# GpSimd's last loop: scatter-adding block b before gathering block b + 4

## What is computed

```python
x = x + xattn(layernorm(x), ctx_1024, ctx_1024, ...)
xf = layernorm(x).reshape(-1, 256)                    # 2048 tokens
top_w, top_idx = top_k(xf @ gate_w, 2)                # two experts per token
combine = zeros((2048, 8)).at[rows, top_idx].add(softmax(top_w))
h = gelu(einsum('td,edf->tef', xf, w1) + b1)          # 8 experts, 256 -> 1024
y = einsum('tef,efd->ted', h, w2) + b2                # 1024 -> 256
x = x + einsum('ted,te->td', y, combine)
```

## Time and profile before

| | |
|---|---|
| time before, median of 3 runs | 368.38 us (356.95, 368.38, 372.02) |
| the profiled execution's own time | 358.27 us |
| its span | 356.5 us |
| busy in the span | TensorE 316.4, VectorE 260.8, ScalarE 236.4, GpSimd 174.2 us |
| the 39 scatters on GpSimd (L486) | 64.8 us busy, 109.6 us idle just before them |
| the 39 gathers on GpSimd (L479) | 41.3 us busy, 37.4 us idle just before them |
| DMA queues, share of 16 engines' span | q1 (SyncE) 52.5%, q0 (GpSimd) 17.3% |

### The profile page before, as it was taken

The page is one execution under the profiler, slowest core; times in us unless marked ns, Lnnn a source line. Parts: engine busy times, 40 slices in busy tenths (PEclk is TensorE's granted clock), DMA queues, the critical chain, the costliest instruction groups (busy, mean ns, idle before and its releaser), DMA issues.

```text
span 356.5 us, 11376 instructions
## 1 busy us (share of the span) xinstructions
PE 316.4 (89%) x3919; PEld 289.6 (81%) x3919; DVE 260.8 (73%) x604; ACT 236.4 (66%) x543; POOL 174.2 (49%) x189
## 2 busy tenths in 40 slices
PE   6589888889977999999999899999989999999940
PEld 4478787888867999998999789889889899999930
DVE  8989998971798888877778767777768765666600
ACT  1589989972333688877888858678777564656510
POOL 7878989942103154444544453535442635444231
PEclk9999999975786999999999999999999999999985
DMA  7899999999411068598787876877777778778221
GB/s 232 267 348 330 351 352 334 330 392 322 159 10 46 17 167 279 176 278 251 204 258 205 268 182 202 235 244 202 244 205 233 223 233 220 246 217 267 37 29 15
DMA packets 34096, 78.52 MB, mean 220 GB/s; under 512 B 10437, under 2 KB 23945, under 8 KB 27514
## 3 DMA queue, kind: packets, MB, share of 16 engines
q1 hardware_dynamic: 24088, 66.72, 52.5%
q0 software_dynamic: 7600, 10.48, 17.3%
q10 hardware_dynamic: 2354, 0.59, 0.7%
HBM read 31.07 MB, written 9.64 MB: 114 GB/s over the span
## 4 chain that ended last, share of the span: by engine, by line
PE 58%; DVE 8%; DMA 8%; issue 6%; ACT 3%; POOL 2%; POOLq 1%; DVEq 0%; ACTq 0%
PE bank L1090 25%; PE bank L1105 23%; DMA out<-shared,row_of 6%; PE bank L1066 2%; DVE W L874 1%; PE bank L1007 1%; PE bank L1031 1%; DVE shared L926 1%; DMA shared<-xn_rows,row_of 1%; PE bank L1057 1%; PE bank L963 1%; PE bank L1107 1%; PE bank L988 1%; PE bank L957 1%; PE bank L996 1%
## 5 line engine op out<-in xcount | busy, mean ns | idle before, releaser
L486 POOL DMA_INDIRECT out<-shared,row_of x39 | 64.8, 1662 | 109.6 <-DMA out<-shared,row_of 74.6
L1105 PE MATMUL bank<-W,shared 128*128 (+1 forms) x936 | 108.5, 273 | 0.0
L1090 PE MATMUL bank<-shared,XR 128*128 128x128 f16 x1680 | 99.9, 218 | 5.0 <-issue 4.0
L1090 PEld LDWEIGHTS bank<-shared,XR 128*128 128x128 f16 x1680 | 95.8, 97 | 8.4 <-issue 8.0
L1105 PEld LDWEIGHTS bank<-W,shared 128*128 128x128 f16 x936 | 89.9, 98 | 9.8
L604 ACT ACTIVATE shared<-shared 128x512 f32<-128x512 f32 x78 | 49.1, 629 | 53.4 <-DVE shared L926 53.0
L945 DVE SCALAR_TENSOR_TENSOR shared<-shared,XP 128x512 f16<-128x512 f32 x70 | 52.4, 749 | 25.8 <-ACT shared L606 25.3
L926 DVE SCALAR_TENSOR_TENSOR shared<-bank,XP 128x512 f32<-128x512 f32 x70 | 52.5, 750 | 24.1 <-PE bank L1090 20.3
L479 POOL DMA_INDIRECT shared<-xn_rows,row_of x39 | 41.3, 1059 | 37.4 <-DVE w_of L941 14.0
L606 ACT ACTIVATE shared<-shared,XP 128x512 f16<-128x512 f32 x70 | 50.6, 723 | 2.3
L874 DVE SCALAR_TENSOR_TENSOR W<-W,wscale (+1 forms) x32 | 40.8, 1280 | 2.9 <-ACT W L538 1.5
(11 more groups left out here) (169 smaller groups left out, 422.2 us busy)
## 6 DMA issues: line engine op xcount, KB each, us to landing
XR<-W SPq DMA_DIRECT2D x35, 1024.0 KB
W<-in_w SPq DMA_DIRECT2D x16, 1024.0 KB, 7.5
shared<-in_ctx_t SPq DMA_DIRECT2D x16, 256.0 KB, 5.2
W<-in_ctx SPq DMA_DIRECT2D x16, 128.0 KB, 6.3
out<-XR SPq DMA_DIRECT2D x16, 128.0 KB, 6.3
xn_rows<-W SPq DMA_DIRECT2D x16, 128.0 KB, 6.4
XR<-in_x SPq DMA_DIRECT2D x3, 512.0 KB, 7.3
shared<-xn_rows,row_of POOLq DMA_INDIRECT x39, 4.2
```

Source lines behind the costliest of these rows:

```text
L486: pool.indirect_dma_start(out=out, out_offset=bass.IndirectOffsetOnAxis(ap=row_of[:, b:b + 1], axis=0), in_=Y[:, b % 2, :], in_offset=None ...
L1090: mm = pe.matmul(pHT[n][m][:, f % 4, :], first[:, c, w, f * P:(f + 1) * P], XT[:, n, v, c, :], start=(c == 0 and w == 0 and v == 0), stop= ...
L1105: pe.matmul(pY[n], hT[:, n, v, f, :], whole(Wh[:, slot, at:at + D]), start=(f == 0 and w == 0 and v == 0), stop=False)
```

## The change

In GpSimd's loop the two halves of the body change places. At each index i the scatter of block i - 2 is now issued first, and the gather of block i + 2 after it. Both keep their waits. In terms of blocks, the gather of block b + 4 used to come ahead of the scatter of block b (and behind that of block b - 1), and now comes behind the scatter of block b.

```diff
             for i in range(-2, NB + 2):
-                b = i + 2
-                if b < NB:
-                    after(pool, gt_ok, b - 2)
-                    after(pool, got_w, b - 2)
-                    pool.indirect_dma_start(out=XG[:, b % 3, :], out_offset=None, in_=xn_dram,
-                                            in_offset=bass.IndirectOffsetOnAxis(ap=row_of[:, b:b + 1], axis=0))\
-                        .then_inc(xg_ok[b % 3], 16)
                 b = i - 2
                 if 0 <= b:
                     after(pool, added, 16 * b)
                     pool.wait_ge(ys_ok, b + 1)
                     pool.indirect_dma_start(out=out,
                                             out_offset=bass.IndirectOffsetOnAxis(ap=row_of[:, b:b + 1], axis=0),
                                             in_=Y[:, b % 2, :], in_offset=None, compute_op=ALU.add,
                                             bounds_check=ROWS - 1, oob_is_err=True).then_inc(added, 16)
+                b = i + 2
+                if b < NB:
+                    after(pool, gt_ok, b - 2)
+                    after(pool, got_w, b - 2)
+                    pool.indirect_dma_start(out=XG[:, b % 3, :], out_offset=None, in_=xn_dram,
+                                            in_offset=bass.IndirectOffsetOnAxis(ap=row_of[:, b:b + 1], axis=0))\
+                        .then_inc(xg_ok[b % 3], 16)
```

## The result

The changed kernel is slower by a quarter: 458.98 us in the median of 4 runs (450.18 to 465.96), against 363.01 us (356.95 to 372.02, 4 runs). The ratio to the kernel before is 1.264, with a 95% interval of 1.245 to 1.284. The forecast was 369.5 us and the range 359 to 384.

The account below looks back on a forecast made before the run. The prediction took TensorE to bound the block loop. Steady stage +5.9, start +3.4 and end -3.1 us sum to +6.2 us, which on the median of 363.3 us gives 369.5 us; range 359 to 384.

Parts of the forecast that it names:

- The loop: Transposes, product, Y, scatter, gather behind it, landing, transposes two blocks on: (8.53 + L) / 2, so 6.02 us per block.
- half of the stalls: TensorE's stalls, 0.25 us a block, would add 0.125 if all stayed; half was taken, giving 6.08 us a block.
- The landing, L: Time from a gather's issue to its landing, meeting the first part of the next copy: taken as 3.5 us.
- The prediction's own sign of being wrong, a landing over 4: In the block loop, a gather's landing over 4 us would show the forecast wrong.
- The rival with L at 4.2 us: Gather latency sets the block loop's pace in full: +16.6 to +20.3 us, about 5% slower; chance 0.25.
- the fit of the Trainium skill: GpSimd-issued DMA takes 2.0 us plus bytes over 436 GB/s: gather 2.3 us, no cost in the steady stage.
- The reaction: GpSimd's step from Y done to the scatter's issue: 0.29 us.
- The clock: Rival: waits of 0.2 to 0.5 us a block lower TensorE's clock for a tenth of the stage, +19 us; chance 0.03.
- The start: Blocks up to 7: block 7's transposes come at 149.17 against 145.80 before, +3.4 us.
- The end: Last scatters no longer lag: the last one 16.60 us after the last transposes, 19.69 before, -3.1 us.
- Faster: Rival: TensorE's stalls vanish under the waits in the block loop, -2.2 us, at most -8 us; chance 0.05.
- The loop stays slack: Rival: landings of 3.1 us, 5.82 us a block, TensorE keeps its pace, within 3 us of before; chance 0.17.

Follow-up runs that it names:

- nobounds: The changed kernel with the scatter's bounds check left out: 456.21 us, ratio 1.256.
- hold: The changed kernel with SyncE's 1 MB copy of w1 held back until the scatter of four blocks before has landed: 404.44 us, ratio 1.116.
- fill: The changed kernel with 48 small unused matmuls on TensorE ahead of the transposes of every even block from 4 on: 434.83 us, ratio 1.196.
- both: The changed kernel with the held copy and the filler matmuls together: 416.15 us, no ratio.

## Why the prediction was wrong

**The bound and the loop were right.** The loop, its seven steps, its unit of two blocks, and that the scatters all but stop waiting for each other and land faster (3.8 us in the median, 5.0 before) came as written. The profile shows the landing of the scatters:

```profile
DMA to landing us min/median/max: 3.7/3.8/6.7
```

**What the gather meets, and what the wait does to the clock, were wrong, all to one side.** The prediction had 12.03 us for two blocks, plus 0.12 for half of the stalls. The turn followed above has 16.84:

| term | predicted | measured |
|---|---|---|
| transposes to bias matmul | 5.53 | 7.97 (246.41 to 254.38) |
| bias matmul to Y done | 0.78 | 0.79 |
| Y done to scatter | 0.29 | 0.89 (255.17 to 256.06) |
| scatter to gather | 1.89 | 1.89 |
| gather's landing, and start | 3.54 | 5.30 |

*The landing, L.* This is the step that failed first. The text took L = 3.5 for a gather issued "some 0.7 us ahead of the next copy", which "meets its first part". No run bears that out. The late gathers of the changed kernel take 5.3 to 5.8 us, those of nobounds that go out 0.45 to 0.76 us ahead of the copy 5.7 to 6.1: they land with the copy. The prediction's own sign of being wrong, a landing over 4, was met. The price 3.5 came from the gathers of 253.38 and 322.89 in the kernel before (3.4 and 3.7), said to have "the nearest" surroundings. The copies behind those two show that they had not:

```profile
255.60 0.49 SPq L371 DMA_DIRECT2D XR<-W  x1
325.98 0.49 SPq L371 DMA_DIRECT2D XR<-W  x1
```

They went out 2.2 and 3.1 us behind the gathers, not 0.7. The rival with L at 4.2 us was too low as well. The run hold, in which the copies go out 2.0 us or more behind most gathers again, shows that the copy is the cause (3.0 to 3.1 us in the turns shown), and takes the ratio from 1.264 to 1.116, more than half of the loss.

The phase was off too, but that made no difference. I had stretched each iteration by the forecast wait; the wait stands ahead of every second transposes only, and the other iteration begins 0.10 us after the product. So the scatter goes out 1.58 us into it (254.48 to 256.06), not 0.5 to 0.7.

By the fit of the Trainium skill that the prediction names, an estimated 2.3 us of landing would have made the change free in the steady stage. The least landing here is 2.8 us in the changed kernel, and 5.3 beside a copy of SyncE. "DMA: Bandwidth & Descriptors" of the Trainium skill, section "Queues, rings and completion order", says that each DMA engine takes turns between the queues that have work for it, a packet at a time. The runs agree in this much, that a gather on q0 isn't served ahead of a copy on q1 that is in flight beside it, even where the gather was issued first: 5.3 to 5.8 us, against 3.0 to 3.1 in the turns of hold.

*The reaction.* I took 0.29 us from one row at the end of the kernel before. That scatter (343.48) wasn't set off by its Y alone: in the chain that ended last the scatter before had landed at 342.64, 0.84 us ahead of it, and GpSimd was already on its way when Y was done at 343.19. In the steady stage of the changed kernel it needs 0.89 us from Y to scatter, 0.56 of it as "issue" ahead of its last semaphore. This term is 0.6 us too small, but since the gather lands with the copy whether it goes out some tenths earlier or later, no run shows that it cost anything in the changed kernel; where the copy is out of the way, as in hold, it counts in full.

*The clock.* I gave it 3%, as a rival by itself, for pauses of 0.2 to 0.5 us. The pauses are 3.5 us, since the gather lands so late. TensorE's part of the loop grows by 2.44 us. Of these 1.6 are the slower w1 matmuls (4.45 us, 2.86 before), and the run fill took them away and with them some 20 us. The other 0.8 us are the later start of the w1 matmuls, 1.05 us after the transposes in place of 0.22. It is there in fill as well, so it isn't the clock; its cause is open. The prediction had let half of such stalls vanish under the new waits. The run both shows that copy and clock are no sum of independent cases: I should have put them into one rival in which one brings on the next.

*The start.* Predicted +3.4 us up to block 7, measured +13.7: the first turn is long already (block 4's transposes come 10.87 us after block 3's).

*The end.* Predicted -3.1 us, measured +0.5. In hold and fill the last scatter comes 17.56 and 17.76 us after the last transposes, 19.69 in the kernel before, so 2 us are gained there and the mechanism was right. In the changed kernel it takes 20.18: its last w1 matmuls follow a wait and are slow.

*The chances.* Slower had 0.40, no change 0.55. The range came from the median landing and bounded it by no collision, although the prediction itself quoted landings up to 5.2 us for gathers and 6.8 for scatters. Small slips change nothing: with L = 3.1 the start would be +2.6 and not +3.0, and the idle time in the earlier trace rows is 5.2 and not 5.4 us. The fit of the Trainium skill, an estimated 5.42 us a block by the loop, would end at TensorE's own 5.64 and so under "Faster", not under "The loop stays slack".

## What to carry to other kernels

A prefetch that is issued behind a result's write inherits every wait of that result, and closes a loop through the engine that it feeds. Work out the loop in the order in which the consumer really runs: where it carries over two iterations, one of them starts late and the other on time, and the transfer's phase against others must be taken for the one that starts on time. Here a small gather issued within a microsecond of a 1 MB copy landed only when the copy did, whichever of the two went first; so price a transfer by what is in flight when it goes out *and* by what goes out just behind it. When a loop comes out within a microsecond of the bound, treat its wait, the collision it moves into and the clock that falls in the wait as one case and not as three, since the collision made the wait here and the wait brought down the clock.

## What the runs showed of the hardware

- After waits of 2.9 us and more the granted clock was lower for some microseconds (0.67 and 0.73 over 5.6 us in the stretch shown) and 48 matmuls took 4.3 to 4.5 us in place of 2.86, but for one iteration with 4.0. After the shorter waits of the run hold they mostly took 2.85, but in 3 of 17 iterations 4.5 to 5.3. Filling the wait with unused matmuls made the kernel faster (458.98 to 434.83 us in the medians).
- A gather of 132 KB landed in 2.8 to 4.3 us in the run hold from block 6 on, 3.1 in the median, with the next 1 MB copy 2.0 us or more behind it. In the changed kernel, with such a copy on the other queue issued from 0.22 us ahead of it to 0.5 us behind it, it landed in 5.3 to 5.8 us (once 7.7), for the most part within 0.5 us behind the copy.
- The 0.56 us that GpSimd spends between the semaphore of Y and the scatter's issue are not the bounds register's: without it they are 0.54.
